# A third window buffer, taps and output scales by way of DRAM, and new instruction orders in a fused attention, convolution and expert kernel

## What is computed

```python
# x: 32 samples x 32 channels x 512 steps, f32; T = 32 channels
agg_w = einsum('bk,koi->boi', att, weight)              # att: softmax of a small net on cond (32 x 8)
h = einsum('boi,bih->boh', agg_w, x) + agg_b[:, :, None]
q, k, v = (bitnet_linear(h, w, s) for w, s in ...)      # sign(w), row scale s * mean|w|
x = x + bitnet_linear(attention(q, k, v), o_weight, o_scale)   # 32 heads of 16, 8 k/v heads
c = conv1d(x, weight, width 9, 4 groups) + ctx + bias   # along the 512 steps
flat = c.reshape(-1, 512)
w = top-2 gates of softmax(flat @ router_w.T + router_b)
x = x + (einsum('nd,erd->ner', flat, A) * w) @ Bm * 0.5
```

## Time and profile before

| | us |
|---|---|
| three runs | 126.24, 127.68, 130.19 (median 127.68) |
| profiled execution: device time | 126.31 |
| its span, first to last instruction | 124.5 |
| around the span | 1.8 |

### The profile page before, as it was taken

The page is one execution under the profiler, slowest core; times in us unless marked ns, Lnnn a source line. Parts: engine busy times, 40 slices in busy tenths (PEclk is TensorE's granted clock), DMA queues, the critical chain, the costliest instruction groups (busy, mean ns, idle before and its releaser), DMA issues. The chain is left out here.

```text
span 124.5 us, 2544 instructions
## 1 busy us (share of the span) xinstructions
PE 110.4 (89%) x876; PEld 85.6 (69%) x876; DVE 93.8 (75%) x254; ACT 63.6 (51%) x139; POOL 46.3 (37%) x57
## 2 busy tenths in 40 slices
PE   0469999999999999999999999999999469599870
PEld 0357799999979898988885788585767126257510
DVE  0067699969899999779899988975576828278852
ACT  4585499999176954364767256454342103103510
POOL 1116100006039733649996897787120000000000
PEclk9999999999999999999999999999999999999997
DMA  3899999910000000004900258499899939992232
GB/s 82 270 358 411 407 403 408 386 50 3 0 5 0 0 0 5 3 0 158 184 0 0 84 121 206 149 206 184 205 205 197 216 137 211 187 303 109 87 140 113
DMA packets 18174, 19.28 MB, mean 155 GB/s; under 512 B 944, under 2 KB 13936, under 8 KB 17776
## 3 DMA queue, kind: packets, MB, share of 16 engines
q1 hardware_dynamic: 17008, 17.01, 52.4%
q10 hardware_dynamic: 1152, 2.10, 4.8%
HBM read 14.91 MB, written 4.19 MB: 153 GB/s over the span
## 5 line engine op out<-in xcount | busy, mean ns | idle before, releaser
L360 POOL TENSOR_TENSOR probs<-probs,row_inv 128x512 f32<-128x512 f32 x16 | 16.8, 1050 | 15.1 <-DVE row_inv L890 9.7
L1254 PE MATMUL bank<-mixed_hi,qkv_sign 128*128 128x256 f32 x72 | 17.8, 289 | 0.1
L1255 PE MATMUL bank<-mixed_lo,qkv_sign 128*128 128x256 f32 x72 | 17.0, 278 | 0.0
L342 POOL TENSOR_TENSOR keys_diag<-kv,keymask 128x512 f32<-128x512 f32 x8 | 8.3, 1039 | 16.0 <-DVE calm L859 15.9
L1254 PEld LDWEIGHTS bank<-mixed_hi,qkv_sign 128*128 128x128 f32 x72 | 13.5, 188 | 0.7 <-DVE scale_v L760 0.2
L1255 PEld LDWEIGHTS bank<-mixed_lo,qkv_sign 128*128 128x128 f32 x72 | 13.6, 188 | 0.0
L1332 PE MATMUL bank<-wo_sign,attn_hi 128*128 128x512 f32 x32 | 13.2, 412 | 0.0
L500 ACT ACTIVATE probs<-probs 128x512 f32<-128x512 f32 x16 | 9.8, 627 | 6.2 <-DVE probs L880 6.2
L1332 PE MATMUL bank<-wo_sign,attn_lo 128*128 128x512 f32 x32 | 12.6, 394 | 0.0
L506 ACT ACTIVATE probsT<-bank 128x512 f32<-128x512 f32 x16 | 9.5, 596 | 5.9 <-PE bank L1308 5.7
L1347 PE MATMUL bank<-rows_sb,conv_w_sb 96*32 96x512 f32 x64 | 8.6, 605 | 4.1 <-DMA rows_sb<-x_turned 4.1
(11 more groups left out here) (144 smaller groups left out, 233.2 us busy)
## 6 DMA issues: line engine op xcount, KB each, us to landing
rows_sb<-x_turned SPq DMA_DIRECT2D x24, 256.0 KB, 5.3
x_all<-in_x_rows SPq DMA_DIRECT2D x4, 512.0 KB, 9.2
x_turned<-x_all ACTq DMA_DIRECT2D x8, 256.0 KB, 4.3
out_rows<-x_all SPq DMA_DIRECT2D x8, 256.0 KB, 2.1
qkvT_sb<-in_qkvT SPq DMA_DIRECT2D x4, 384.0 KB, 5.9
rows_sb<-in_qkv_rows SPq DMA_DIRECT2D x1, 1536.0 KB, 10.4
rows_sb<-in_wo_rows SPq DMA_DIRECT2D x1, 1024.0 KB, 13.9
woT_sb<-in_woT SPq DMA_DIRECT2D x1, 1024.0 KB, 17.0
```

The lines of the kernel that those rows point to most:

```text
L360: pool.tensor_tensor(probs[:, t % 2, h, :, :], probs[:, t % 2, h, :, :], row_inv[:, t % 2, h, :].unsqueeze(2).to_broadcast([P, HALF, TOKENS]),
L1254: mm(dst, w, mixed_hi[:, ph, cols(i % 2, PAIR)], start=(ph == 0 and n % 2 == 0), stop=False)
L1255: last = mm(dst, w, mixed_lo[:, ph, cols(i % 2, PAIR)], start=False, stop=(ph == PHASES - 1 and n % 2 == 1))
```

## The change

- **Windows.** A third window lies in `qkv_sign`, free once the last projection is done; POOL clears its edges in `clear_third`. Tile t uses window t % 3, and `to_window(t)` waits for the convolution of tile t-3. SP issues the output store of tile 0 between the windows of tiles 5 and 6.
- **Taps.** `conv_in`, the mask, the 12 products and the copy are gone. SP loads the taps right into `conv_w_sb` with 48 DMAs of 8 x 32 numbers (1 KB each).
- **Output scales.** The diagonal, the product and the copy are gone. SP stores 128 x 4 numbers to DRAM and reads them back into all partitions.
- **Late sums.** DVE adds x to y for the last two tiles, not for the last alone.
- **Bias in halves.** The product with ones that spreads the mixing bias contracts 32 rows, the lower for tiles 0 to 3 and the upper for tiles 4 to 7, where it contracted 64.
- **Orders.** All five lists are written anew in places.

```diff
+        x1_win.append(qkv_sign[0:WINDOW, :, :].rearrange("p a n -> p (a n)")[:, 0:win_w].bitcast(F32)
+                      .rearrange("p (s g m) -> p s g m", s=PER_TILE, g=CONV_GROUPS))
@@ SP
-            sp.dma_start(conv_in[:, :, :], conv_w).then_inc(in_conv, 16)
+            def load_taps():
+                for shift in range(3):
+                    for ph in range(PHASES):
+                        for g in range(CONV_GROUPS):
+                            own = conv_w[ph * TOKENS + g * MEMBERS_IN:ph * TOKENS + (g + 1) * MEMBERS_IN, shift, :]
+                            sp.dma_start(conv_w_sb[TOKENS * shift + ph:TOKENS * (shift + 1):PHASES, g, :],
+                                         own.rearrange("c (q g o) -> c q g o", q=PHASES, g=CONV_GROUPS)[:, :, g, :]
+                                         ).then_inc(in_conv, 16)
+            def spread_o_scale():
+                sp.wait_ge(scale_ready, 2)
+                sp.dma_start(o_scale_dram.rearrange("(a c) -> c a", c=P), scale_all[:, BLOCKS:],
+                             allow_slow_non_contiguous=True).then_inc(o_scale_stored, 16)
+                sp.wait_ge(o_scale_stored, 16)
+                sp.dma_start(o_scale_bc[:, :], o_scale_dram.partition_broadcast(P)).then_inc(o_scale_ready, 16)
             def to_window(t):
                 sp.wait_ge(x1_stored[t], 16)
-                reached(sp, conv_done, t - 1)
+                if t == 2:
+                    sp.wait_ge(win_cleared, 6)
+                reached(sp, conv_done, t - 2)
-            for t in range(TILES):
-                to_window(t)
-            for t in range(TILES):
-                store(t)
+            load_taps()
+            spread_o_scale()
+            to_window(0)
...
+            to_window(5)
+            store(0)
+            to_window(6)
+            to_window(7)
+            store(1)
...
+            store(7)
@@ DVE
-                v.tensor_tensor(o_diag.rearrange("p (a n) -> p a n", a=PHASES),
-            def keep_o_scale():
-            def keep_conv_weights():
             def bound_o():
-                dve.wait_ge(o_scale_ready, 1)
+                dve.wait_ge(o_scale_ready, 16)
-            def residual_last():
-                t = TILES - 1
+            def residual_late(t):
                 dve.wait_ge(y_scaled, t + 1)
@@ PE
-                mm(ps_aggb[0][:, PAIR:], ones[0:TILES * MIXES, :], bias_columns(slice(2, 4)), start=True, stop=True)
-                mm(ps_aggb[1][:, :], ones[0:TILES * MIXES, :], bias_columns(slice(4, TILES)), start=True,
+                bias_of(ps_aggb[0][:, PAIR:], slice(2, 4))
+                bias_of(ps_aggb[1][:, :], slice(4, TILES)).then_inc(aggb_done, 1)
-            def spread_o_scale():
-            def gather_conv():
             def convolve(t):
-                pe.wait_ge(windowed[t % 2], 48 * (t // 2 + 1))
+                pe.wait_ge(windowed[t % 3], 48 * (t // 3 + 1))
```

More of the change, by code:

```diff
@@ L1132, in _ @@
             bias_conv(4)
+            finish(1)
             bias_conv(5)
-            finish(1)
             gate_top(3)
@@ L1154, in _ @@
             gate_weights(6)
+            finish(5)
             gate_apply(6)
-            finish(5)
             gate_top(7)
@@ L1194, in spread_shares, with bias_of @@
                 mm(bank[4][0:TILES * MIXES, 0:PER_TILE], own, spread[:, 0:P:TOKENS], start=True, stop=True).then_inc(att_done, 1)
-            def bias_columns(tiles):
-                return outer_b[:, tiles, :, :].rearrange("p t q o -> p (t q o)")
+            def bias_of(out, tiles):
+                half = TILES * MIXES // 2
+                rows = slice(0, half) if tiles.stop <= TILES // 2 else slice(half, 2 * half)
+                return mm(out, ones[rows, :], outer_b[rows, tiles, :, :].rearrange("p t q o -> p (t q o)"), start=True, stop=True)
             def mix_bias_first():
                 pe.wait_ge(outer_b_ready, 1)
-                mm(ps_aggb[0][:, 0:PAIR], ones[0:TILES * MIXES, :], bias_columns(slice(0, 2)), start=True,
-                   stop=True).then_inc(aggb_done, 1)
+                bias_of(ps_aggb[0][:, 0:PAIR], slice(0, 2)).then_inc(aggb_done, 1)
             def mix_bias_rest():
@@ L1269, in total_bound @@
                 mm(ps_bound[0:1, 0:PAIRS + 4], ones[:, 0:1], sums[:, :], start=True, stop=True).then_inc(bound_done, 1)
-            def spread_o_scale():
-                pe.wait_ge(qkv_copied, BLOCKS + 2)
-                pe.wait_ge(o_diag_ready, 1)
-                mm(ps_o_scale[:, :], ones[:, :], o_diag, start=True, stop=True).then_inc(o_scale_done, 1)
-            def gather_conv():
-                pe.wait_ge(in_conv, 16)
-                pe.wait_ge(conv_rows_ready, 1)
-                pe.wait_ge(mixed_full, 2 * PAIRS)
-                taps = conv_in[:, :, :].rearrange("p sh (q g o) -> p sh g q o", q=PHASES, g=CONV_GROUPS)
-                for shift in range(3):
-                    for g in range(CONV_GROUPS):
-                        last = mm(ps_conv_w[TOKENS * shift:TOKENS * (shift + 1), TOKENS * g:TOKENS * (g + 1)],
-                                  conv_rows[:, TOKENS * g:TOKENS * (g + 1)], taps[:, shift, g, :, :], start=True, stop=True)
-                last.then_inc(conv_w_done, 1)
             def score(t):
@@ L1347, in convolve @@
                     last = mm(ps_conv(t)[TOKENS * g:TOKENS * (g + 1), :], conv_w_sb[:, g, :],
[L1348 removed]
+                              x1_win[t % 3][:, :, g, 1:1 + STEPS], start=True, stop=True)
                 last.then_inc(conv_done, 1)
@@ L1480, in _ @@
             ffn_up(4)
+            ffn_down(3)
             ffn_up(5)
-            ffn_down(3)
+            turn_conv(6)
+            turn_gated(4)
             convolve(7)
-            turn_gated(4)
-            turn_conv(6)
             ffn_down(4)
```

337 lines of the change are left out of this document (167 added, 170 removed).

## The result

The changed kernel took **135.47 us** (median of four runs, 134.43 to 135.71), the kernel before 127.06 beside it (four runs, 126.24 to 130.19). The ratio is 1.067, with a 95% interval of 1.056 to 1.078: slower, and far outside the range of the prediction. Any of these kernels has a slow execution now and then (130.19 here), and the ratios leave these out. The profiled execution took 135.32 us, its span 133.5 against 124.5.

The account below looks back on a forecast made before the run. PE sets the pace from 30 to 90 us, window transfers at the end. 1.8 off PE and 4.07 idle, of which 0.8 stays, give 5.1: span 119.4, time 121.2, forecast put at 121.9; range 119.8 to 126.4.

Parts of the forecast that it names:

- gain of PE ahead of the middle: PE arrives at the tail about 1.8 us earlier: 1.6 from removed products, 0.2 from the bias product.
- bias in halves: On PE, contracting 32 rows instead of 64 gains between nothing and 0.53 us; 0.2 taken.
- window 6 issued: SP issues tile 6's window at 95.5 us, where it was 101.1, through an earlier sum and store.
- window 7 landed: Tile 7's window lands at 106.5 us, after its store takes 6.4 at worst and its read 5.8.
- idle time before the last convolutions: PE's 4.07 us of waiting for windows before the last four convolutions falls to 0.8.
- The taps: On SP, 48 tap issues at 0.49 us take 23.5 us, from 13.7 to 37.2, hidden before the first window.
- The output scales: Store and read take some 7 us, at the quick end of 3.6 to 7.6 each; whole at 44, 6 us cover.
- The sign to look for: Forecast wrong if `bound_o` waits on a DMA or a tap issue costs SP above 0.61 us.
- The rival: Taps hold up DVE: none issued until inputs land at 27.4, scales 7.7 us late, 129.6 us; chance 0.10.
- The tail: Following tiles 6 and 7 from store to window, tile 7's convolution starts at 106.5 instead of 111.33 us.
- DVE did not become the bound: Rival: PE's 1.8 us turn into waits for softmax halves on DVE, giving 123.7 us; chance 0.12.
- the windows crowd: Rival: DMA engines move stores no faster than windows, window 7 lands at 109 or beyond, 124.4 us; chance 0.14.

Follow-up runs that it names:

- the run with the quick store: Changed kernel with the output scales stored as 128 pieces of 16 bytes, 48 taps kept; 127.25 us in the quicker of two runs.
- all mends: Changed kernel with taps in one DMA, output scales stored in 16-byte pieces and the bias product over 64 rows again; 122.12 us, ratio 0.968.
- the first experiment: Changed kernel with the taps laid out ready in DRAM and loaded by one DMA in place of 48; 121.28 us, ratio 0.961.
- the scales first: Changed kernel with SP's store and read of the output scales put ahead of the 48 taps; 134.13 us in the quicker of two runs.

## Why the prediction was wrong, step by step

| Step of the prediction | Forecast | Measured |
|---|---|---|
| taps begin on SP | 13.7 | 10.4 |
| 48 taps take SP | 23.5 | 37.8 |
| store and read of the scales | 7 | 13.3 |
| `o_scale_bc` whole | 44 | 61.5 |
| `bound_o` asks | 50.2 | 49.0 |
| gain of PE ahead of the middle | 1.8 | 1.35 (taps in one DMA: 1.5; in twelve: 1.9) |
| bias in halves | 0.2 | -0.2 (taps in one DMA: -0.1; in twelve: 0.4) |
| window 6 issued | 95.5 | 96.1 (taps in one DMA) |
| window 7 issued | 100.7 | 97.6 (taps in one DMA) |
| window 7 landed | 106.5 | 105.9 (taps in one DMA) |
| last convolution | 106.5 | 106.6 (taps in one DMA) |
| idle time before the last convolutions | 0.8 | 0.46; taps in one DMA: 0.17 |
| span | 119.4 | 119.3 (taps in one DMA); 133.5 |

**The step that failed** is the one called "The taps": 48 issues at 0.49 us, a price taken from the window reads the earlier trace rows. A tap took 0.67, with stalls 0.79. That row was the wrong neighbour: a window read fills 32 partitions, a tap 8, and the smaller transfer was the dearer to issue. The second wrong term was "The output scales", where I took the quick end, 3.6 us, twice. The store took 8.3, beyond even the slow end of 7.6 that I had as the bound; a store in 4-byte pieces has no neighbour among reads in 512-byte runs. The read took 4.9, inside the bounds. The two errors add on the one path, but they don't weigh the same. With the forecast's 0.49 per tap, the scales would have been there at 10.4 + 23.5 + 13.3 = 47.2, before `bound_o` asked at 49.0, slow store and all. With its 7 us for the scales and the taps as they were, they come at 10.4 + 37.8 + 7 = 55.2, 6.2 too late; the run with the quick store waits 5.5. So the taps' price alone breaks the forecast, and the scales' makes it worse. In sum: 37.8 - 23.5 = 14.3 for the taps and 6.3 for the scales make 20.6, less 3.3 for the earlier start, so the scales came 17.3 us later than forecast. Of that, 4.8 was cover (49.0 less 44.2), and 12.5 was DVE's wait.

**The sign to look for was named and was right.** The prediction gave 0.61 us per tap as the point where the cover is gone, and a wait of `bound_o` on a DMA as what would show it. But I then judged whether a tap could cost 0.61 by a row of another kind. With two unmeasured terms in series in front of every engine, 6 us of cover and 48 repetitions, an error of 0.12 us in one issue was enough. A chance of 0.10 for this rival was too small by much.

**The rival had the right place and the wrong cause.** It said that no tap would go out until the inputs had landed at 27.4. In the changed trace 16 of the 48 had been started by 24 us. The stall of 3.67 us on the last input moved onto a tap: the last input's issue takes 0.43 now, and the first tap takes 3.1 (the 3145 above). Behind the loads the 48 taps took 3.5 us more than behind the scales, not 14. The rival too had 7 us for the scales and 0.49 per tap. Its 129.6 us fell short because its wait was 7.7 us and not 12.5, and because it left out what the idle time does to the clock, 2.2 us.

**What held, and where it was luck.** The tail was worked out by following the two last tiles from store to read. With the taps in one DMA the stores of tiles 6 and 7 left at 89.03 and 94.55 (forecast 89.4 and 94.3), and window 6 went out within 0.7 us of the forecast. But the store of tile 7 landed in 2.2 us and not in 6.4, so window 7 went out 3 us early; its reads took up to 7.3 us and not 5.8, and it was there at 105.9. The last convolution started at 106.64 with no idle time before it: PE's own list set that start, not the window that the forecast followed, so that the two agree to 0.1 us is in part luck. The same holds for the span of 119.3 against 119.4: 0.3 us less gained ahead of the middle and 0.6 less idle time left at the end cancel in part. The parts, each from its own experiment: the early stores and the late sum 2.8, PE's products 1.6, and the third window 1.6 where the new orders are in. They add to more than the 5.2 found, so they overlap. DVE did not become the bound where the middle ran undisturbed: PE is 1.5 us ahead there at 53 us. Nor did the windows crowd to a cost: with the taps in one DMA no convolution of the last four waits for one, though the reads of window 7 were slow.

**The best version** is the changed kernel with the taps in one DMA, 121.28 us, or with twelve, 121.30: 3.9% under the kernel before. No run tells these two, or the one with all mends (122.12), apart. All of these need the taps laid out ahead of time, which the 12 products did on the chip. Where that is not allowed, taps on PE and scales through DRAM (121.86), or 48 taps and scales on PE (122.43), give nearly the same.

## What to carry to other kernels

A DMA issue is an instruction of the engine that issues it. Multiply its price by the count, take the price from a DMA of the same shape, and add it up to the next thing in that queue that somebody waits for; if no row has that shape, forecast with the slow end when the queue has little cover. Two slow things that are each hidden can still fail together, so the cover has to be tested against their sum. And when a single short wait holds an engine that feeds all others, its price is the idle time plus the slower clock behind it.

## What the runs showed of the hardware that I had not expected

- The tap loads were dearer to issue than far larger DMAs. SP's issues of 8 rows took 0.62 to 0.67 us, whether 1 or 4 KB; window reads of 32 rows mostly 0.30 to 0.49; the last inputs over 128 rows mostly 0.43 to 0.5; the broadcast read to 128 partitions 0.33. Smallness alone isn't it, as the store of the scales, 2 KB, took 0.34 to 0.44. Why was not tested.
- A store of 512 single numbers takes 8.3 to 8.8 us to land, with the DMA engines idle or nearly so; as 128 pieces of 16 bytes it takes 1.4 to 1.5.
- The stall of about 3 us falls on the fifth issue from the load of `in_wo_rows` on, whatever that is: the last input before (3.67), the first tap of the change (3.1), the single tap DMA of 48 KB in the first experiment (3.26). Where nothing was issued there, with the scales first, no tap took longer than 0.84.
- After 11.5 us of idle time the granted clock of PE was 0.50 for 60 to 70 us, and work that took 3.04 us at a clock of 1.00 in the kernel before took 5.23; from 40 to 50 us it had been 1.00 here too.
- Two products of 32 rows, one on the lower and one on the upper rows, took 1.05 to 1.15 us in seven of ten traces, where two of 64 rows took 1.48 to 1.52.
